# Probabilities divided on VectorE instead of GpSimd, and GELU of three gates after their eviction

## The chip, the cores and the metric

The kernel runs on one core of one Trainium2 chip. The metric is the device time of one execution in microseconds (us). Before the change the median of three executions is 2908.08 us (2890.9 to 2912.65). The kernel's engines are TensorE (PE; PEld is its weight load), VectorE (DVE), ScalarE (ACT), GpSimd (POOL) and SyncE (SP), which issues nearly all DMAs.

## The reference

The program computes four residual steps on 4 batches of 512 tokens with 128 features each: attention with 16 small heads, a stack of six layers, a second attention, and a routed mixture of experts. The change lies in the stack of layers (`DEPTH = 6`). What a layer computes, cut to what matters:

```
for i in range(DEPTH):
    x = attn_layer(shift_tokens(x), Wqkv[i], q_scale[i], k_scale[i], Wo[i]) + x
    x = ffn_layer(shift_tokens(x), ln_g[i], ln_b[i], W1[i], b1[i], W2[i], b2[i]) + x

attn_layer: q, k, v = split(x @ Wqkv)              # 16 heads of 64
            q = l2norm(q) * qs;  k = l2norm(k) * ksc
            q, k = rotated with cos, sin and a scale by position
            sim = q @ k.T * 8 within a window of 32 tokens and the one ahead of it
            out = softmax(sim) @ v;  return out @ Wo
ffn_layer:  xn = layernorm(x) * g + bln
            a, gate = split(xn @ W1 + b1)          # 341 columns each
            return a * gelu(gate, exact) @ W2 + b2
```

## The kernel before

**Tiles, slots and rounds.** In the layers the work is cut into tiles T of 128 tokens: four tiles (`TILES`) make one batch entry, four entries one layer, so 6 x 4 x 4 = 96 tiles. Every engine runs a list of 96 *slots*, one for each tile, written out by hand (`layer_slots`): the slots of the first two entries and of the last two stand alone, the 16 slots of a layer between them are the body of a loop that runs five times. Here the four slots of one entry are called a *round*, and slot 0 to slot 3 are its slots by `i`. The engines meet through semaphores that count up.

**What a slot does.** In slot T the attention of tile T is scored while tile T+1 is rotated and normalised, tile T+2 is projected and tile T-1 is weighed. By engine, in program order:

- PE: turns the keys and queries of tile T (`turn_keys`, `turn_queries`, L866, L881), mixes values (L929), `scores(T)` (mask L888, scores L898), projects tile T+2 (L855), mixes again, `weigh(T-1)` (L919, reads the turned probabilities in `sc`), `turn_windows` (L911).
- DVE: `square_sums(T+1)` (L1552, L1553), `turn_probs(T-1)` (L1601, a transpose of 128x1024), `turn_plain(T+1)` (L1558, waits for both products of `turn_swapped(T+1)` on POOL), `add_queries(T+1)` (L1563), `softmax(T)` (L1579 the maxima, L1584 the difference, both read PSUM), `scaled(T+1, 0)` (L1573), `sums(T)` (L1589 and the reciprocal L1594), `scaled(T+1, 1)` (L1573).
- ACT: copies keys and queries (L1284, L1288), `guess(T+1)` (L1276, L1279, after L1553), `exponentials(T)` (L1292, after L1584), `take(T+2)` (L1262, two halves out of PSUM), `squares(T+2)` (L1270), `weighed(T-1)` (L1301), `windows` (L1306).
- POOL: a small copy (L606), `inverse_root(T+1)` (L585 to L588, after the guess), `add_keys(T+1)` (L593), `normalise(T)` (L598, waits for the reciprocal L1594), `turn_swapped(T+2)` (L576, L577, waits for `take(T+2)`).

Two tiles of probabilities lie in `sc[:, 0]` and `sc[:, 1]`; the turned ones in `sc[:, 2]`.

**The feed-forward part** of an entry is spread over the slots of a round two rounds later. PE multiplies three chunks of gate columns (`gate`, L958; chunk 0 at the end of slot 0, chunks 1 and 2 in slot 1 ahead of `scores`) into one and the same PSUM bank 7, so each waits until ACT has evicted the one before. ACT evicts them with the GELU itself (L1323), and the table of functions is switched for it and back (ACT_TABLE_LOAD, L1323 and L1361 in slot 0, L1323 and L1344 in slot 1). The three plain chunks (`plain`, L966) follow through the same bank, each waiting for DVE's `hidden` of the one before (L1639): `plain(0)` and `plain(1)` in slot 1 ahead of and behind `weigh`, `plain(2)` in slot 2 ahead of `scores`. On DVE `hidden(0)` and `hidden(1)` close slot 1, `hidden(2)` stands ahead of `softmax` in slot 2, whose end holds L1644 and L1621; slot 0 has the layer norm's scale (L1629, L1633) behind `softmax`, slot 3 its centring (L303). `gate(1)` and `gate(2)` stand on ACT behind `guess`.

Of the kernel before, what the change touches and what calls it, by code (L numbers as in the profile page):

```python
# [20 lines left out]
P = 128  # L21
# [57 lines left out]
def build(nc, I, out):  # L79
    with ExitStack() as ctx:  # L80
# [3 lines left out]
        def sem(name):  # L84
            return ctx.enter_context(nc.semaphore(name))
# [119 lines left out]
        def projections(a, b):  # L205
# [42 lines left out]
            sem(n) for n in ("l_xt", "l_xe", "l_px", "l_pc", "l_mm", "l_mw", "l_m", "l_res", "l_xf", "l_fn"))  # L248
        f_h, f_g, f_hd, f_y = sem("f_h"), sem("f_g"), sem("f_hd"), sem("f_y")

# [275 lines left out]
        def _(pool):  # L526
# [67 lines left out]

            def normalise(T, i):
                pool.wait_ge(l_rd, T + 1)
                p3 = probs(i).rearrange("p (h j) -> p h j", j=64)
                pool.tensor_tensor(p3, p3, rden(i).unsqueeze(2).broadcast_to([P, LH, 64]), ALU.mult).then_inc(l_pn, 1)  # L598

            def slot(it, l, b, i, ahead):  # L600
# [6 lines left out]
                if ahead >= 1:  # L607
                    inverse_root(T + 1, (i + 1) % 2)
                    add_keys(T + 1, (i + 1) % 2)
                normalise(T, i)  # L610
                if ahead >= 2:
# [38 lines left out]
        def _(pe):  # L650
# [263 lines left out]
            def weigh(T, i):  # L914

                p4 = sc[:, 2, :].rearrange("p (h v t) -> p h v t", h=LH, v=2)
                for half in range(2):
# [218 lines left out]
        def _(act):  # L1136
# [183 lines left out]
            def gate(j, n):  # L1320
                m = FCH[n][1]
                act.wait_ge(f_h, 6 * j + n + 1)
                act.activation(gates[0:m, n, :], bank[0:m, 7, :], ACT.Gelu, bias=lb[0:m, 6 + n:7 + n]).then_inc(f_g, 1)  # L1323

# [5 lines left out]
            def slot(it, l, b, i, ahead):  # L1330
# [10 lines left out]
                if i == 1 and feeds:  # L1341
                    gate(it - 2, 1)
                    gate(it - 2, 2)
                    act.preload_act_table_set("natural_log_exp_and_others")  # L1344
                exponentials(T, i)
# [13 lines left out]
                if i == 0 and feeds:  # L1359
                    gate(it - 2, 0)  # L1360
                    act.preload_act_table_set("natural_log_exp_and_others")  # L1361
                if i == 0 and not (isinstance(it, int) and it == LAST):
# [23 lines left out]
            for n in range(3):  # L1386
                gate(LAST - 1, n)
            act.preload_act_table_set("natural_log_exp_and_others")
            shift_ffn(LAST, BATCH - 1)
            ln_squares(act, LAYER0 + LAST)  # L1390
            layer_root(LAST)
            for n in range(3):
                gate(LAST, n)
            act.preload_act_table_set("natural_log_exp_and_others")
            attention(1)
# [22 lines left out]
        def _(dve):  # L1418
# [168 lines left out]
            def sums(T, i):  # L1587
# [6 lines left out]
                dve.reciprocal(rden(i), u_den).then_inc(l_rd, 1)  # L1594

            def turn_probs(T, i):
                if not (isinstance(T, int) and T == 0):
                    dve.wait_ge(l_px, 2 * T)
                dve.wait_ge(l_pn, T + 1)
                settle(dve)  # L1600
                dve.transpose(sc[:, 2, :], probs(i)).then_inc(l_pt, 1)  # L1601

# [32 lines left out]
            def hidden(j, n):  # L1635
                m = FCH[n][1]
                dve.wait_ge(f_h, 6 * j + n + 4)
                dve.wait_ge(f_g, 3 * j + n + 1)
                dve.scalar_tensor_tensor(out=hT[0:m, n, :], in0=bank[0:m, 7, :], scalar=lb[0:m, 3 + n:4 + n],  # L1639
# [7 lines left out]
            def slot(it, l, b, i, ahead):  # L1647
# [5 lines left out]
                if ahead >= 1:  # L1653
                    square_sums(T + 1, (i + 1) % 2)
                if not (first and i == 0):
                    turn_probs(T - 1, (i - 1) % 2)
                if ahead >= 1:
# [14 lines left out]
                if ahead >= 1:  # L1672
                    scaled(T + 1, (i + 1) % 2, 1)
                if i == 1 and feeds:
                    hidden(it - 2, 0)
                    hidden(it - 2, 1)
# [12 lines left out]
            layer_slots(dve, slot)  # L1689
            turn_probs(DEPTH * BATCH * TILES - 1, 1)  # L1690
            scale_norm(LAST - 1, DEPTH - 1)
# [168 lines left out]
```

## Time and profile before

| | before |
|---|---|
| median of three executions | 2908.08 us (2890.9 to 2912.65) |
| the profiled execution | 2895.91 us, span 2894.1 us |
| busy: PE, DVE, ACT, POOL | 2220.3, 1948.6, 1536.6, 1470.0 us |
| granted TensorE clock, mean | 0.893 |
| slots of the layers, first to last reciprocal | 423 to 2248 us of the span |

The layers are about 1830 us of the span, the rest belongs to the two attentions and the experts, which the change leaves alone. A row of a timeline gives start and length in us, engine, line, operation, output<-input, the count of merged instructions, and in brackets the engine's idle time before it with what ended it.

### The profile page before, as it was taken

The numbers are of one execution on the slowest core, as the hardware profiler recorded it, in microseconds if no ns is written. First come the engines' busy times: TensorE is split into PE (matmuls) and PEld (weight loads), VectorE is DVE, ScalarE is ACT, GpSimd is POOL, SyncE is SP. The second block draws the span as 40 slices with busy tenths as digits, with TensorE's granted clock in tenths as the row PEclk, the third lists the DMA queues.
The fourth block names the chain that finished last, engine by engine and source line by source line (L and its number), as shares of the span: only waits on it lengthen the run. The fifth ranks groups of instructions, "written<-read, shape, count | busy, mean of one in ns | idle before, by whom it ended". The sixth has DMA issues, their size and how long they took to land.

```text
span 2894.1 us, 53763 instructions
## 1 busy us (share of the span) xinstructions
PE 2220.3 (77%) x21684; PEld 1186.8 (41%) x21780; DVE 1948.6 (67%) x2087; ACT 1536.6 (53%) x1859; POOL 1470.0 (51%) x1031
## 2 busy tenths in 40 slices
PE   4678758788888888888888888888888756788253
PEld 1111124455555455545555555545555311112253
DVE  2676457888778878787778887887877246763101
ACT  2255745665666666656656665666665223546100
POOL 5500047776676667666667766766766153000202
PEclk8698989999999999999999999999999766989686
DMA  5100000000010000000010001000000010000122
GB/s 154 50 21 26 1 1 16 1 2 16 1 25 2 16 1 10 16 16 1 1 25 1 16 2 25 2 16 1 9 2 1 0 60 32 23 23 16 41 76 65
DMA packets 55828, 59.08 MB, mean 20 GB/s; under 512 B 13142, under 2 KB 45012, under 8 KB 55508
## 3 DMA queue, kind: packets, MB, share of 16 engines
q1 hardware_dynamic: 53444, 50.77, 5.9%
q0 software_dynamic: 2128, 4.72, 0.7%
q8 instruction: 182, 2.98, 0.5%
q14 instruction: 74, 0.61, 0.1%
HBM read 44.07 MB, written 11.01 MB: 19 GB/s over the span
## 4 chain that ended last, share of the span: by engine, by line
PE 47%; issue 13%; ACT 13%; POOL 12%; DVE 11%; DMA 2%; SPq 1%; POOLq 0%; ACTq 0%; DVEq 0%
PE bank L855 7%; PE bank L929 6%; PE bank L919 5%; PE bank L731 5%; PE bank L702 4%; DVE big L1452 3%; PE bank L898 3%; ACT pxs L1301 2%; POOL big L576 2%; POOL big L593 2%; ACT L1323 2%; PE bank L958 2%; POOL big L577 2%; ACT big L1176 2%; PE bank L966 2%
## 5 line engine op out<-in xcount | busy, mean ns | idle before, releaser
L598 POOL TENSOR_TENSOR sc<-sc,small 128x1024 f32<-128x1024 f32 x96 | 263.4, 2744 | 467.3 <-DVE small L1594 467.3
L1452 DVE TENSOR_REDUCE big<-bank 128x1 f32<-128x512 f32 x512 | 328.6, 685 | 199.1 <-PE bank L702 194.8
L1292 ACT ACTIVATE sc<-sc 128x1024 f32<-128x1024 f32 x96 | 101.5, 1057 | 532.2 <-DVE sc L1584 532.2
L855 PE MATMUL bank<-wqk,xs 128*128 128x512 f32 x768 | 364.8, 617 | 13.4 <-ACT xs L1257 8.3
L929 PE MATMUL bank<-pxs,mw 128*128 128x256 f32 x1536 | 366.2, 382 | 0.0
L929 PEld LDWEIGHTS bank<-pxs,mw 128*128 128x128 f32 x1536 | 291.1, 192 | 100.9 <-issue 70.3
L1176 ACT ACTIVATE big<-bank 128x1024 f32<-128x1024 f32 x256 | 250.1, 1026 | 139.6 <-PE bank L716 136.8
L1558 DVE TENSOR_TENSOR big<-big,rotCl 128x2048 f32<-128x2048 f32 x96 | 222.4, 2317 | 79.2 <-POOL big L577 79.2
L702 PE MATMUL bank<-pxs 48*128 48x512 bf16 x512 | 186.1, 445 | 116.1 <-DVE big L1452 72.1
L1552 DVE TENSOR_REDUCE small<-big 128x32 f32<-128x2048 f32 x96 | 219.0, 2281 | 38.2 <-ACT big L1270 28.5
L1573 DVE TENSOR_TENSOR big<-big,small 128x1024 f32<-128x1024 f32 x192 | 241.0, 1256 | 1.1 <-POOL small L588 1.1
L919 PE MATMUL bank<-sc,xnat 32*128 32x512 f32 x1536 | 200.8, 637 | 41.9 <-ACT big L1262 39.0
L576 POOL TENSOR_TENSOR big<-big,rotSl 128x1024 f32<-128x1024 f32 x96 | 226.9, 2364 | 8.3 <-ACT big L1262 8.2
L577 POOL TENSOR_TENSOR big<-big,rotSl 128x1024 f32<-128x1024 f32 x96 | 227.5, 2370 | 0.0
L593 POOL TENSOR_TENSOR big<-big 128x1024 f32<-128x1024 f32 x96 | 226.2, 2356 | 0.0
L1579 DVE TENSOR_REDUCE small<-bank 128x16 f32<-128x1024 f32 x96 | 116.9, 1218 | 142.5 <-PE bank L898 142.5
L855 PEld LDWEIGHTS bank<-wqk,xs 128*128 128x128 f32 x768 | 142.6, 196 | 168.1 <-issue 160.9
L1301 ACT ACTIVATE pxs<-bank 128x1024 f32<-128x1024 f32 x192 | 185.7, 1020 | 39.9 <-PE bank L919 36.5
L958 PE MATMUL bank<-xc,w 128*128 128x512 f32 x144 | 102.4, 800 | 119.4 <-ACT gates L1323 116.5
L1270 ACT ACTIVATE big<-big 128x2048 f32<-128x2048 f32 x96 | 183.3, 1910 | 11.5 <-DVE small L1553 1.1
L1262 ACT ACTIVATE big<-bank 128x1024 f32<-128x1024 f32 x192 | 184.8, 1011 | 5.3 <-PE bank L855 5.2
L702 PEld LDWEIGHTS bank<-pxs 48*128 48x128 bf16 x512 | 40.5, 95 | 356.4 <-DVE big L1452 267.7
(237 smaller groups left out, 4035.4 us busy)
## 6 DMA issues: line engine op xcount, KB each, us to landing
wqk<-in_L_ffn_w SPq DMA_DIRECT2D x32, 256.0 KB, 3.1
wqk<-in_L_ffn_Wqkv SPq DMA_DIRECT2D x12, 512.0 KB, 4.3
pxs<-part_rows SPq DMA_DIRECT2D x64, 96.0 KB
pxs<-part_rows SPq DMA_DIRECT2D x64, 64.0 KB
wvt<-in_wv_layers_t SPq DMA_DIRECT2D x6, 512.0 KB, 5.1
wol<-in_L_ffn_Wo SPq DMA_DIRECT2D x6, 512.0 KB, 5.5
part_rows<-big SPq DMA_DIRECT2D x24, 128.0 KB
part_rows<-sc SPq DMA_DIRECT2D x24, 128.0 KB
```

The lines of the kernel that those rows point to most:

```text
L576: pool.tensor_tensor(r4[:, :, :, 0:h], q4[:, :, :, h:], tab[:, :, :, 0:h], ALU.mult).then_inc(l_rb, 1)
L577: pool.tensor_tensor(r4[:, :, :, h:], q4[:, :, :, 0:h], tab[:, :, :, h:], ALU.mult).then_inc(l_rb, 1)
L593: pool.tensor_tensor(raws(i)[:, INNER:], raws(i)[:, INNER:], rotB[:, INNER:], ALU.add).then_inc(l_ak, 1)
L598: pool.tensor_tensor(p3, p3, rden(i).unsqueeze(2).broadcast_to([P, LH, 64]), ALU.mult).then_inc(l_pn, 1)
L702: pe.matmul(bank[:, 4 + r, :], qst[64 * r:64 * r + MAX_ROW, b % 2, p, qt * P:(qt + 1) * P], kst[64 * r:64 * r + MAX_ROW, b % 2, p, :], sta ...
L855: m = pe.matmul(bank[:, 2 - 2 * half + c, :], xs[:, b % 2, WIN + i * P:WIN + (i + 1) * P], wqk[:, (2 * half + c) * 512:(2 * half + c + 1) ...
L919: m = pe.matmul(bank[:, (4, 5, 2, 3)[w], :], xnat[32 * w:32 * w + 32, i % 2, half, :], p4[32 * w:32 * w + 32, :, half, :], start=(half == ...
L929: m = pe.matmul(bank[:, 6, part * 2 * P:(part + 1) * 2 * P], mw[:, 2 * (a % 4) + s, a // 4, :], pxs[:, part, a, s, :], start=(a == 0 and s ...
L1176: act.activation(pT[:, u % 2, 2 * half:2 * half + 2, :], bank[:, q:q + 2, :], ACT.Exp).then_inc(a_p, 1)
L1301: act.activation(pxs[:, i // 2, :, :, t:t + 64].rearrange("p c r (w t) -> p w (c r) t", w=2), bank[:, 4 - 2 * half:6 - 2 * half, :].rearra ...
L1452: dve.tensor_reduce(nm[:, qt, 2 * p + r:2 * p + r + 1], bank[:, 4 + r, :], AX.X, ALU.max, negate=True).then_inc(a_mx, 1)
L1573: dve.tensor_tensor(r3, r3, nrm(i)[:, half * LH:(half + 1) * LH].unsqueeze(2).broadcast_to([P, LH, LD]), ALU.mult).then_inc((l_yq, l_yk)[h ...
```

## The change

It has two parts. First, `normalise(T)` goes from POOL, where it stood between `add_keys(T+1)` and `turn_swapped(T+2)`, to DVE, behind `scaled(T+1, 1)`; `turn_probs(T)` follows at once, in slot T instead of slot T+1, into one of two buffers (`sc[:, 2 + i % 2]`). Second, ACT evicts each gate chunk with Identity and its bias, without a table switch, and a new function `gelus` applies GELU from SBUF to SBUF to two chunks at once and to the third, between two table loads, in slot 1 behind `gate(2)` and ahead of `exponentials`; `hidden` waits for it by a new semaphore.

```diff
--- before.py
+++ after.py
@@ -246,7 +246,7 @@
             sem(n) for n in ("l_s", "l_mx", "l_e", "l_p", "l_dn", "l_rd", "l_pn", "l_pt"))
         l_xt, l_xe, l_px, l_pc, l_mm, l_mw, l_m, l_res, l_xf, l_fn = (
             sem(n) for n in ("l_xt", "l_xe", "l_px", "l_pc", "l_mm", "l_mw", "l_m", "l_res", "l_xf", "l_fn"))
-        f_h, f_g, f_hd, f_y = sem("f_h"), sem("f_g"), sem("f_hd"), sem("f_y")
+        f_h, f_g, f_ge, f_hd, f_y = sem("f_h"), sem("f_g"), sem("f_ge"), sem("f_hd"), sem("f_y")
 
         m_lg, m_sh, m_ex, m_oh, m_cum, m_ch, m_idx = (
             sem(n) for n in ("m_lg", "m_sh", "m_ex", "m_oh", "m_cum", "m_ch", "m_idx"))
@@ -592,11 +592,6 @@
                 pool.wait_ge(l_rb, 2 * T + 2)
                 pool.tensor_tensor(raws(i)[:, INNER:], raws(i)[:, INNER:], rotB[:, INNER:], ALU.add).then_inc(l_ak, 1)
 
-            def normalise(T, i):
-                pool.wait_ge(l_rd, T + 1)
-                p3 = probs(i).rearrange("p (h j) -> p h j", j=64)
-                pool.tensor_tensor(p3, p3, rden(i).unsqueeze(2).broadcast_to([P, LH, 64]), ALU.mult).then_inc(l_pn, 1)
-
             def slot(it, l, b, i, ahead):
 
                 T = it * TILES + i
@@ -607,7 +602,6 @@
                 if ahead >= 1:
                     inverse_root(T + 1, (i + 1) % 2)
                     add_keys(T + 1, (i + 1) % 2)
-                normalise(T, i)
                 if ahead >= 2:
                     if b == BATCH - 1 and i == 2:
                         pool.wait_ge(l_tab, 3 * l + 6)
@@ -913,7 +907,7 @@
 
             def weigh(T, i):
 
-                p4 = sc[:, 2, :].rearrange("p (h v t) -> p h v t", h=LH, v=2)
+                p4 = sc[:, 2 + i % 2, :].rearrange("p (h v t) -> p h v t", h=LH, v=2)
                 for half in range(2):
                     for w in range(4):
                         m = pe.matmul(bank[:, (4, 5, 2, 3)[w], :], xnat[32 * w:32 * w + 32, i % 2, half, :],
@@ -1320,7 +1314,15 @@
             def gate(j, n):
                 m = FCH[n][1]
                 act.wait_ge(f_h, 6 * j + n + 1)
-                act.activation(gates[0:m, n, :], bank[0:m, 7, :], ACT.Gelu, bias=lb[0:m, 6 + n:7 + n]).then_inc(f_g, 1)
+                act.activation(gates[0:m, n, :], bank[0:m, 7, :], ACT.Identity, bias=lb[0:m, 6 + n:7 + n]).then_inc(f_g, 1)
+
+            def gelus(j):
+
+                act.wait_ge(f_g, 3 * j + 3)
+                settle(act)
+                act.activation(gates[:, 0:2, :], gates[:, 0:2, :], ACT.Gelu).then_inc(f_ge, 1)
+                act.activation(gates[0:FCH[2][1], 2, :], gates[0:FCH[2][1], 2, :], ACT.Gelu).then_inc(f_ge, 1)
+                act.preload_act_table_set("natural_log_exp_and_others")
 
             def mixed_weights(l, half):
                 act.wait_ge(l_mm, 2 * l + half + 1)
@@ -1341,7 +1343,7 @@
                 if i == 1 and feeds:
                     gate(it - 2, 1)
                     gate(it - 2, 2)
-                    act.preload_act_table_set("natural_log_exp_and_others")
+                    gelus(it - 2)
                 exponentials(T, i)
                 if ahead >= 2:
                     take(T + 2, i % 2, 0)
@@ -1358,7 +1360,6 @@
                     layer_root(it - 1)
                 if i == 0 and feeds:
                     gate(it - 2, 0)
-                    act.preload_act_table_set("natural_log_exp_and_others")
                 if i == 0 and not (isinstance(it, int) and it == LAST):
                     if first or second or (isinstance(it, int) and it == 2):
                         act.wait_ge(step_done, LAYER0 + 1)
@@ -1385,13 +1386,13 @@
                 weighed(N - 1, LAST, TILES - 1, half)
             for n in range(3):
                 gate(LAST - 1, n)
-            act.preload_act_table_set("natural_log_exp_and_others")
+            gelus(LAST - 1)
             shift_ffn(LAST, BATCH - 1)
             ln_squares(act, LAYER0 + LAST)
             layer_root(LAST)
             for n in range(3):
                 gate(LAST, n)
-            act.preload_act_table_set("natural_log_exp_and_others")
+            gelus(LAST)
             attention(1)
             norm_all_scalar(act, MOE0)
             act.wait_ge(m_tk, 1)
@@ -1593,12 +1594,17 @@
                 settle(dve)
                 dve.reciprocal(rden(i), u_den).then_inc(l_rd, 1)
 
+            def normalise(T, i):
+                dve.wait_ge(l_rd, T + 1)
+                p3 = probs(i).rearrange("p (h j) -> p h j", j=64)
+                dve.tensor_tensor(p3, p3, rden(i).unsqueeze(2).broadcast_to([P, LH, 64]), ALU.mult).then_inc(l_pn, 1)
+
             def turn_probs(T, i):
-                if not (isinstance(T, int) and T == 0):
-                    dve.wait_ge(l_px, 2 * T)
+                if not (isinstance(T, int) and T < 2):
+                    dve.wait_ge(l_px, 2 * T - 2)
                 dve.wait_ge(l_pn, T + 1)
                 settle(dve)
-                dve.transpose(sc[:, 2, :], probs(i)).then_inc(l_pt, 1)
+                dve.transpose(sc[:, 2 + i % 2, :], probs(i)).then_inc(l_pt, 1)
 
             def tables(l):
 
@@ -1635,7 +1641,7 @@
             def hidden(j, n):
                 m = FCH[n][1]
                 dve.wait_ge(f_h, 6 * j + n + 4)
-                dve.wait_ge(f_g, 3 * j + n + 1)
+                dve.wait_ge(f_ge, 2 * j + (1, 1, 2)[n])
                 dve.scalar_tensor_tensor(out=hT[0:m, n, :], in0=bank[0:m, 7, :], scalar=lb[0:m, 3 + n:4 + n],
                                          in1=gates[0:m, n, :], op0=ALU.add, op1=ALU.mult).then_inc(f_hd, 1)
 
@@ -1652,8 +1658,6 @@
                 more = not (isinstance(l, int) and l == DEPTH - 1)
                 if ahead >= 1:
                     square_sums(T + 1, (i + 1) % 2)
-                if not (first and i == 0):
-                    turn_probs(T - 1, (i - 1) % 2)
                 if ahead >= 1:
                     turn_plain(T + 1, (i + 1) % TILES)
                     add_queries(T + 1, (i + 1) % 2)
@@ -1671,6 +1675,8 @@
                 sums(T, i)
                 if ahead >= 1:
                     scaled(T + 1, (i + 1) % 2, 1)
+                normalise(T, i)
+                turn_probs(T, i)
                 if i == 1 and feeds:
                     hidden(it - 2, 0)
                     hidden(it - 2, 1)
@@ -1687,7 +1693,6 @@
             scaled(0, 0, 0)
             scaled(0, 0, 1)
             layer_slots(dve, slot)
-            turn_probs(DEPTH * BATCH * TILES - 1, 1)
             scale_norm(LAST - 1, DEPTH - 1)
             for n in range(3):
                 hidden(LAST - 1, n)
```

On DVE, at the end of slot 1 (`hidden` writes `hT`; the second L1573 of a slot is `scaled(T+1, 1)`), before:

```order
L1573 TENSOR_TENSOR big<-big,small 128x1024
L1637 ISA
L1638 ISA
L1639 SCALAR_TENSOR_TENSOR hT<-bank,lb,gates 128x512
L1637 REGISTER_ALU
L1638 REGISTER_ALU
L1639 SCALAR_TENSOR_TENSOR hT<-bank,lb,gates 128x512
L1548 REGISTER_ALU
L1552 TENSOR_REDUCE small<-big 128x32
L1553 TENSOR_SCALAR small<-small 128x32
L1601 STREAM_TRANSPOSE sc<-sc 128x1024
```

and now, from the same `scaled(T+1, 1)`, which is L1574 there:

```order
L1574 TENSOR_TENSOR big<-big,small 128x1024
L1600 TENSOR_TENSOR sc<-sc,small 128x1024
L1604 REGISTER_ALU
L1607 STREAM_TRANSPOSE sc<-sc 128x1024
L1643 ISA
L1644 REGISTER_ALU
L1645 SCALAR_TENSOR_TENSOR hT<-bank,lb,gates 128x512
L1643 REGISTER_ALU
L1645 SCALAR_TENSOR_TENSOR hT<-bank,lb,gates 128x512
L1549 REGISTER_ALU
L1553 TENSOR_REDUCE small<-big 128x32
```

The division L1600 and the transpose L1607 (before L1601, behind L1553 of the next slot) stand directly behind the second scaling and ahead of both `hidden`.

On POOL, from `add_keys` to the next small copy, before:

```order
L593 TENSOR_TENSOR big<-big 128x1024
L598 TENSOR_TENSOR sc<-sc,small 128x1024
L568 ISA
L576 TENSOR_TENSOR big<-big,rotSl 128x32x32
L577 TENSOR_TENSOR big<-big,rotSl 128x32x32
L604 ISA
L606 COPY kbuf<-kbuf 128x8x32
```

and now:

```order
L593 TENSOR_TENSOR big<-big 128x1024
L568 ISA
L576 TENSOR_TENSOR big<-big,rotSl 128x32x32
L577 TENSOR_TENSOR big<-big,rotSl 128x32x32
L601 COPY kbuf<-kbuf 128x8x32
```

L598 is gone, so that the two products of `turn_swapped` follow `add_keys` with only their own wait between (L568, for `take`).

On ACT, in slot 1, from the guess (`small`) over the evictions of gate chunks 1 and 2 to the exponentials (`sc`), before:

```order
L1276 ACTIVATE small<-small 128x32
L1279 ACTIVATE small<-small 128x32
L1322 REGISTER_ALU
L1323 ACT_TABLE_LOAD
L1323 ACTIVATE gates<-bank,lb 128x512
L1322 REGISTER_ALU
L1323 ACTIVATE gates<-bank,lb 85x512
L1344 ACT_TABLE_LOAD
L1292 ACTIVATE sc<-sc 128x1024
```

and now:

```order
L1270 ACTIVATE small<-small 128x32
L1273 ACTIVATE small<-small 128x32
L1316 REGISTER_ALU
L1317 ACTIVATE gates<-bank,lb 128x512
L1316 REGISTER_ALU
L1317 ACTIVATE gates<-bank,lb 85x512
L1321 REGISTER_ALU
L1323 ACT_TABLE_LOAD
L1323 ACTIVATE gates<-gates 128x1024
L1324 ACTIVATE gates<-gates 85x512
L1325 ACT_TABLE_LOAD
L1286 ACTIVATE sc<-sc 128x1024
```

The loads now frame the two GELUs behind the last eviction. In slot 0 the two loads around the eviction of chunk 0 (L1323 and L1361) are gone without a replacement.

## Rows read from the trace of the kernel before

**Rows 1.** Busy time of the engines in the layers: stretch, its length, busy us (instructions), granted clock

```profile
core 0: us, PE busy (x) PEld busy (x) DVE busy (x) ACT busy (x) POOL busy (x), PEclk, DMA share, GB/s
420.00:2250.00 1830.00, 1547.99 (x18403) 936.57 (x18497) 1474.02 (x1237) 1144.10 (x1368) 1257.71 (x826) 0.95 0.03 9
```

**Rows 2.** Timeline of DVE in one round, slot 0 to slot 3

```profile
1411.99 1.22 DVE L1579 TENSOR_REDUCE small<-bank 128x16 f32<-128x1024 f32 x1
...
1419.02 1.16 DVE L1573 TENSOR_TENSOR big<-big,small 128x1024 f32<-128x1024 f32 x1
...
1435.76 1.22 DVE L1579 TENSOR_REDUCE small<-bank 128x16 f32<-128x1024 f32 x1 [5.55 <-PE bank L898]
...
1445.70 0.75 DVE L1639 SCALAR_TENSOR_TENSOR hT<-bank,lb,gates 128x512 f32<-128x512 f32 x1 [2.81 <-PE bank L966]
...
1454.16 1.21 DVE L1579 TENSOR_REDUCE small<-bank 128x16 f32<-128x1024 f32 x1
...
1459.45 1.16 DVE L1573 TENSOR_TENSOR big<-big,small 128x1024 f32<-128x1024 f32 x1
1460.53 0.74 DVE L1644 SCALAR_TENSOR_TENSOR zT<-bank,lb,zT 128x512 f32<-128x512 f32 x1
...
1461.91 2.29 DVE L1552 TENSOR_REDUCE small<-big 128x32 f32<-128x2048 f32 x1
...
1464.64 1.23 DVE L1601 STREAM_TRANSPOSE sc<-sc 128x1024 f32<-128x1024 f32 x1
1467.04 2.29 DVE L1558 TENSOR_TENSOR big<-big,rotCl 128x2048 f32<-128x2048 f32 x1 [1.17 <-POOL big L577]
...
1470.51 1.22 DVE L1579 TENSOR_REDUCE small<-bank 128x16 f32<-128x1024 f32 x1
...
1473.05 1.69 DVE L1573 TENSOR_TENSOR big<-big,small 128x1024 f32<-128x1024 f32 x1
...
1476.81 1.16 DVE L1573 TENSOR_TENSOR big<-big,small 128x1024 f32<-128x1024 f32 x1
```

**Rows 3.** Timeline of DVE, the maxima of slot 3 and slot 0, a round later

```profile
1549.56 1.22 DVE L1579 TENSOR_REDUCE small<-bank 128x16 f32<-128x1024 f32 x1
...
1567.10 1.22 DVE L1579 TENSOR_REDUCE small<-bank 128x16 f32<-128x1024 f32 x1
```

**Rows 4.** Timeline of POOL in the same round as rows 2

```profile
1459.62 2.75 POOL L598 TENSOR_TENSOR sc<-sc,small 128x1024 f32<-128x1024 f32 x1 [3.31 <-DVE small L1594]
...
1471.31 2.35 POOL L593 TENSOR_TENSOR big<-big 128x1024 f32<-128x1024 f32 x1
```

**Rows 5.** Timeline of ACT in the same round, slots 1 and 2

```profile
1428.59 0.23 ACT L1279 ACTIVATE small<-small 128x32 f32<-128x32 f32 x1
1428.84 1.28 ACT L1323 ACT_TABLE_LOAD   x1
1430.13 0.69 ACT L1323 ACTIVATE gates<-bank,lb 128x512 f32<-128x512 f32 x1
...
1438.41 1.06 ACT L1292 ACTIVATE sc<-sc 128x1024 f32<-128x1024 f32 x1 [3.52 <-DVE sc L1584]
...
1457.77 1.92 ACT L1262 ACTIVATE big<-bank 128x1024 f32<-128x1024 f32 x2
```

**Rows 6.** Timeline of PE, gate chunk 2 and the scores of slot 1

```profile
1430.88 2.00 PE L958 MATMUL bank<-xc,w 128*85 128x512 f32 x2 [4.30 <-ACT gates L1323]
...
1433.66 2.06 PE L898 MATMUL bank<-kbuf,qT 64*32 64x64 f32 x128
```

**Rows 7.** Timeline of all engines but PE, ahead of the first slot

```profile
404.92 2.34 POOL L593 TENSOR_TENSOR big<-big 128x1024 f32<-128x1024 f32 x1
404.99 6.60 DVE L1573 TENSOR_TENSOR big<-big,small 128x1024 f32<-128x1024 f32 x2 [1.11 <-POOL small L588]
407.43 3.09 POOL L576 TENSOR_TENSOR big<-big,rotSl 128x1024 f32<-128x1024 f32 x1 [0.17 <-POOL big L593]
410.48 3.33 POOL L577 TENSOR_TENSOR big<-big,rotSl 128x1024 f32<-128x1024 f32 x1
```

## The prediction

> **What bounds the kernel now.** I read the busy time of the layers first, then the timelines of DVE, POOL, ACT and PE over one round of four slots. In the layers PE is busy 1548 us of 1830 and DVE 1474 [rows 1]; neither is full, so a loop through several engines sets the pace, and the timeline must show which. I mark a slot by the start of its maxima on DVE (L1579). The round shown has them at 1411.99, 1435.76, 1454.16 and 1470.51 [rows 2]: slot 0 to 1 takes 23.77 us, 1 to 2 takes 18.40, 2 to 3 takes 16.35; slot 3 to 0 takes 17.54 in a later round (1567.10-1549.56) [rows 3]. Together 76.1 us; 24 rounds of that would be 1826, the layers' 1830.
>
> The loop is: reciprocal on DVE, division on POOL (L598, 2.75 us [rows 4]), POOL's two products behind it (L576, L577), then on DVE L1558, which waits 1.17 us for them [rows 2], L1563, the maxima, and so to the next reciprocal. In slot 0 to 1 another wait ends last: DVE waits 5.55 us for the scores [rows 2], PE having waited 4.30 us for the eviction of gate chunk 1 [rows 6], which stood on ACT behind the guess and a table load of 1.28 us [rows 5].
>
> **Part one: the division on DVE.** POOL is relieved of 2.75 us a slot [rows 4]. On DVE the division is like L1573, the same shape with a broadcast factor: 1.16 us [rows 2]. The transpose stays 1.23 us. DVE gains 96 x 1.16 = 111 us of work, and its total in the layers, 1474+111 = 1585, still fits into 1830. The question is what both do to the loop.
>
> POOL's products no longer wait for the division; they wait for `take(T+2)`, which ends in slot 2 at 1457.77+1.92 = 1459.69, that is 5.53 us behind the slot's maxima [rows 2, 5]. With 0.18 us for the semaphore (L576 idled 0.17 us behind L593's end [rows 7]) L576 is ready at +5.71. Just there DVE runs the second L1573 (+5.29 to +6.45 in slot 2, +6.30 in slot 3, +7.03 in slot 0 [rows 2]) and then the division. All three read two operands from SBUF, and the trace shows that such operations of DVE and POOL exclude each other. Ahead of the first slot two L1573 stand back to back while POOL has L593, L576 and L577 to do [rows 7]: the two take 6.60 us instead of 2.3, L576 3.09 and L577 3.33 instead of 2.35. The ends fit one order only: L593 to 407.26, L1573 to about 408.33, L576 to 410.52, L1573 to 411.59, L577 to 413.81. So they take turns, an operation waiting on one engine goes in between two of the other, a blocked product ends 2.19 us behind the release (410.52-408.33) and a blocked L1573 1.07 us (411.59-410.52). The 1.69 us of L1573 at 1473.05, beside L593 [rows 2, 4], is the same in small (1473.66+1.08).
>
> The Trainium skill (SBUF — State Buffer, section "SBUF: two separate sides") says that a VectorE operation with two SBUF inputs and a GpSimd operation that reads SBUF lock each other out for a whole instruction. The trace agrees, with the 6.60 us.
>
> So, counted from the maxima, with 0.17 us between division and transpose and the pipeline's small overlaps:
>
> - *Slot 2 to 3.* L1573 to 6.45, L576 in between to 8.64, division to 9.71, transpose to 11.1, L1644 and L1621 1.38 (1461.91-1460.53) to 12.5, L1552 and L1553 2.6 (2.73 before, 1464.64-1461.91, with L576 of POOL beside them), then 3.47 from L1558 to the maxima (1470.51-1467.04): 18.5, before 16.35. POOL's L577 ends at 11.9 and is waited for no more.
> - *Slot 3 to 0.* L576 is first (5.71 to 8.06), L1573 to 9.13, L577 to 11.3, division to 12.4, transpose to 13.8, 2.6 and 3.47: 19.8, before 17.54.
> - *Slot 1 to 2.* As slot 2 up to the transpose at 11.1; `hidden(0)` to 11.8; only then PE can run `plain(1)`, for which I take 1.1 (half of what gate chunk 2 took after idle time, 2.00 [rows 6]); `hidden(1)` to 13.7; 2.6, 3.47 and `hidden(2)` 0.7: 20.3, before 18.40. The wait of 2.81 us in front of the second L1639 [rows 2] shrinks, but is not gone.
> - The eight slots of the first two rounds have no gates and less beside them. Between nothing and slot 2's +2.2 I take +1.5 each, 12 us in all.
>
> Without these locks the same sums give 16.5, 16.1 and 18.4: even then the DVE, now serial, would gain little in slots 1 and 2.
>
> **Part two: the gates.** In slot 0 ACT loses two loads of 1.28 us; it then stands idle instead, since the guess waits for L1553. With the division in front, slot 0 runs: L576 from 5.71, L1573 (due at 7.03) to 9.13, L577 to 11.3, division 12.4, transpose 13.8, L1552 and L1553 to 16.4. Then the guess (two short ACTIVATEs, 0.23 us one [rows 5]) to 17.1, and the eviction of chunk 1 (0.69, no load ahead of it) to 17.85. From its end to the maxima the rows give 1435.76-1430.82 = 4.94 us [rows 2, 5], with PE slow after its idle time (2.00 us for two matmuls of chunk 2, 2.06 for the scores [rows 6]); PE idles about as long again, so I keep it: 22.8, before 23.77. Of the 3.85 us of loads that left this chain 1.0 is kept, the division's way has taken the rest. The GELUs follow the last eviction: 1.28, 1.06 (as the exponentials of the same size, L1292), 0.69 and 1.28 make 4.3 us, and the eviction itself 0.69. From the end of gate chunk 2 (1432.88) to L1292 (1438.41) there are 5.53 us [rows 5, 6]; they hide there, and would cost exponentials and all behind them up to 1.5 us if the scores ran at the full clock.
>
> The load's price is where the page and the row differ. Behind the load of 1.28 us the eviction starts at once, 1430.13 after 1428.84+1.28 [rows 5]. The Trainium skill (ScalarE: Activation LUTs, section "What ACT_TABLE_LOAD costs") adds a drain of about 1380 ns to each switch; with it the load ahead of chunk 1 would be worth 1.4 us more, 30 us over 22 rounds. The row decides: 1.28.
>
> **The sum.** A round goes from 76.1 to 22.8+20.3+18.5+19.8 = 81.4. That is +5.3; a few rounds are longer than the one shown (24 x 76.1 stays 4 us under 1830) and have some cover of their own, so I take +5. 22 rounds with gates: +110; the first two: +12. Profiled execution 2896+122 = 3018. The median of before lies 12 us above that execution; I say 3020.
>
> **Rivals.**
> 1. *Faster.* The locks don't bite: L576 gets ready only after the division (it would have to come 1.9 us later, beyond +7.6), or DVE is served first. For it: POOL's start is by a hop from another place. Against it: rows 7. Round: 16.5+16.1+18.4, and slot 0 with its division done at 9.35 gives 19.8: 70.8, -5.3; times 22, with a few for the start: 2775. If only every second lock bites (DVE passes both its operations at one turn) about 2830. Chance 17%.
> 2. *Nearly nothing.* The gates give more: PE's gap ahead of chunk 2 gets short enough that it stays at the full clock, 1.8 us less a round, and one of the three lock terms is lost: 81.4-1.8-2.2 = 77.4, +29 us over 22 rounds: 2930. Chance 11%.
> 3. *Slower still.* PE idles 282 of 1830 us now and would idle about 400 of 1950, and its clock, 0.95 as a mean in the layers [rows 1], falls; the scores of slot 1 were slow after an idle time of 4.30 us [rows 6]. If slots 0 and 1 lose 1 to 2 us each to it: 3065 to 3100. Or slots 1 and 2 fall into the order of slot 3, their L1573 only 0.42 us ahead of L576: +2.2 each, 3115. Chance 14%.
>
> The forecast itself, 2940 to 3050, has 58%. The range, 2860 to 3090, leaves out most of rival 1 and the far end of rival 3. Differences under 1% (2879 to 2937) are about what a measurement can't tell from none: faster 0.17, same 0.11, slower 0.72.
>
> **What would show it.** Each step has its row: the division on DVE with 2.2 to 3.3 us instead of 1.16; L576 starting some 5.7 us behind the maxima and L577 or L576 at about 3.3; slots of 22.8, 20.3, 18.5, 19.8; no wait of DVE for L577; ACT idle ahead of the guess of slot 1; the second `hidden` waiting about 1 us. A division of 1.2 us throughout would make it wrong at its main step.

## The result and the profile after

The changed kernel takes 2990.47 us as a median (2984.79 to 3002.68, four executions), the kernel before 2903.66 in its four: a ratio of 1.031, 95% interval 1.026 to 1.036. The forecast was 3020 (2860 to 3090), slower. The profiled execution took 2984.79 us with a span of 2983.0, 88.9 more than before.

The layers, in the view that answers to [rows 1] (stretch, length, busy us and instructions of each engine, granted clock):

```profile
core 0: us, PE busy (x) PEld busy (x) DVE busy (x) ACT busy (x) POOL busy (x), PEclk, DMA share, GB/s
420.00:2337.00 1917.00, 1576.81 (x18472) 959.62 (x18471) 1741.62 (x1330) 1118.18 (x1364) 1115.20 (x735) 0.93 0.03 9
```

VectorE is busy 1742 us where it was busy 1474. That is 268 more for 96 divisions which, at their own length (1.21 us in a run below), are worth 116. The groups in the page's list (busy us, mean ns of one) tell where the rest lies:

```profile
L1600 DVE TENSOR_TENSOR sc<-sc,small 128x1024 f32<-128x1024 f32 x96 | 319.7, 3331 | 0.0
L1574 DVE TENSOR_TENSOR big<-big,small 128x1024 f32<-128x1024 f32 x192 | 292.2, 1522 | 1.1 <-POOL small L588 1.1
L577 POOL TENSOR_TENSOR big<-big,rotSl 128x1024 f32<-128x1024 f32 x96 | 319.4, 3328 | 0.0
L576 POOL TENSOR_TENSOR big<-big,rotSl 128x1024 f32<-128x1024 f32 x96 | 264.6, 2756 | 311.4 <-ACT big L1256 311.2
```

Of the kernel before:

```profile
L1573 DVE TENSOR_TENSOR big<-big,small 128x1024 f32<-128x1024 f32 x192 | 241.0, 1256 | 1.1 <-POOL small L588 1.1
L1553 DVE TENSOR_SCALAR small<-small 128x32 f32<-128x32 f32 x96 | 98.1, 1022 | 3.3
```

The divisions hold 320-116 = 204 us of it, and the scalings (L1574) 51 us more than before. The total grows by less than that, because a small operation, L1553 (now L1554), fell from 98 to 18 us: a collision that the kernel before had is gone. Its rows in slot 0 of the round in [rows 2], DVE and then POOL, show that it ends with GpSimd's first product:

```profile
1422.40 1.86 DVE L1553 TENSOR_SCALAR small<-small 128x32 f32<-128x32 f32 x1
```

```profile
1421.90 2.33 POOL L576 TENSOR_TENSOR big<-big,rotSl 128x1024 f32<-128x1024 f32 x1
```

In the kernel before, 91 of the 96 L1553 take over 0.3 us (0.18 where nothing holds one), and 89 of these end 0.03 to 0.05 us behind the end of one of GpSimd's operations on `big`. So a second SBUF tensor is not the only thing that makes a VectorE operation collide: this one reads one tensor and two constants.

The timeline of slot 2 of the changed kernel, DVE and then POOL (L1580 is the maxima, before L1579; L1574 the second scaling, before L1573), answers to [rows 2, 4]:

```profile
1509.59 1.22 DVE L1580 TENSOR_REDUCE small<-bank 128x16 f32<-128x1024 f32 x1
...
1514.91 1.16 DVE L1574 TENSOR_TENSOR big<-big,small 128x1024 f32<-128x1024 f32 x1
1515.99 3.37 DVE L1600 TENSOR_TENSOR sc<-sc,small 128x1024 f32<-128x1024 f32 x1
1519.50 1.25 DVE L1607 STREAM_TRANSPOSE sc<-sc 128x1024 f32<-128x1024 f32 x1
...
1527.78 1.22 DVE L1580 TENSOR_REDUCE small<-bank 128x16 f32<-128x1024 f32 x1
```

```profile
1515.21 3.06 POOL L576 TENSOR_TENSOR big<-big,rotSl 128x1024 f32<-128x1024 f32 x1 [2.90 <-ACT big L1256]
1518.23 3.34 POOL L577 TENSOR_TENSOR big<-big,rotSl 128x1024 f32<-128x1024 f32 x1
```

L576 arrives at +5.62 behind the maxima, while L1574 runs to 1516.07 (+6.48). It ends at 1518.27, the division at 1519.36 (+9.77), L577 at 1521.57. The prediction had 5.71, 6.45, 8.64, 9.71 and 11.9 for these.

Between the maxima of slot 0 and slot 1 the gates' part shows, on ACT and on PE of the changed kernel (L1270 and L1273 are the guess, L1317 the evictions, L952 gate chunk 2, L892 the scores), which answers to [rows 5, 6]:

```profile
1482.96 0.23 ACT L1270 ACTIVATE small<-small 128x32 f32<-128x32 f32 x1 [2.87 <-DVE small L1554]
1483.31 0.23 ACT L1273 ACTIVATE small<-small 128x32 f32<-128x32 f32 x1
1483.45 0.67 ACT L1317 ACTIVATE gates<-bank,lb 128x512 f32<-128x512 f32 x1
...
1486.99 1.28 ACT L1323 ACT_TABLE_LOAD   x1
1488.29 1.06 ACT L1323 ACTIVATE gates<-gates 128x1024 f32<-128x1024 f32 x1
1489.25 0.61 ACT L1324 ACTIVATE gates<-gates 85x512 f32<-85x512 f32 x1
1489.88 1.28 ACT L1325 ACT_TABLE_LOAD   x1
1491.18 1.06 ACT L1286 ACTIVATE sc<-sc 128x1024 f32<-128x1024 f32 x1
```

```profile
1484.17 2.00 PE L952 MATMUL bank<-xc,w 128*85 128x512 f32 x2 [3.78 <-ACT gates L1317]
1485.97 1.06 PE L882 MATMUL bank<-maskr,maskw 128*128 128x512 bf16 x2
1486.95 1.48 PE L892 MATMUL bank<-kbuf,qT 64*32 64x64 f32 x128
```

The load ahead of chunk 1 is gone, yet PE idles 3.78 us for it, after 4.30 before. The guess in front of the eviction comes no earlier, although ACT has lost the two loads of slot 0: it ends 17.0 us behind the maxima before and 16.9 now (means of 22 rounds). Before, ACT itself was late; VectorE's sum of squares, which the guess needs, had ended at 12.2. Now that sum ends at 16.2, behind the blocked division, and ACT stands idle for it (2.87 us in the first row).

The time of a slot, from one start of the maxima to the next, worked out from the starts of all 96 (means over the 21 whole rounds from the third one on):

| slot | before | after | change | predicted |
|---|---|---|---|---|
| 0 to 1 | 23.75 | 21.36 | -2.4 | -1.0 |
| 1 to 2 | 19.03 | 22.09 | +3.1 | +1.9 |
| 2 to 3 | 16.60 | 18.35 | +1.8 | +2.2 |
| 3 to 0 | 18.34 | 19.99 | +1.6 | +2.3 |
| round | 77.7 | 81.8 | +4.1 | +5.3, taken as +5 |

21 rounds make +85 us, the first eight slots +4.6, the last three +2.2: 92. What lies around the layers is 3 us shorter in the after trace, which I leave as the difference of two executions.

### The profile page after: what moved, and what is told of

The parts are those of the page before. It is cut to its first block and busy times, and to the rows that moved or that the text cites. A ratio compares the mean times of both kernels' runs of the same rounds, so it can differ in the third digit from the quotient of the medians.

```text
span 2983.0 us, 53967 instructions
## 1 busy us (share of the span) xinstructions
PE 2249.5 (75%) x21780; PEld 1207.7 (40%) x21780; DVE 2216.0 (74%) x2183; ACT 1517.6 (51%) x1863; POOL 1323.4 (44%) x935
## 5 line engine op out<-in xcount | busy, mean ns | idle before, releaser
L576 POOL TENSOR_TENSOR big<-big,rotSl 128x1024 f32<-128x1024 f32 x96 | 264.6, 2756 | 311.4 <-ACT big L1256 311.2
L1600 DVE TENSOR_TENSOR sc<-sc,small 128x1024 f32<-128x1024 f32 x96 | 319.7, 3331 | 0.0
L577 POOL TENSOR_TENSOR big<-big,rotSl 128x1024 f32<-128x1024 f32 x96 | 319.4, 3328 | 0.0
L1574 DVE TENSOR_TENSOR big<-big,small 128x1024 f32<-128x1024 f32 x192 | 292.2, 1522 | 1.1 <-POOL small L588 1.1
L913 PE MATMUL bank<-sc,xnat 32*128 32x512 f32 x1536 | 210.6, 665 | 71.8 <-ACT big L1256 69.7
L585 POOL TENSOR_TENSOR small<-small 128x32 f32<-128x32 f32 x96 | 125.7, 1310 | 268.3 <-ACT small L1273 268.3
L1553 DVE TENSOR_REDUCE small<-big 128x32 f32<-128x2048 f32 x96 | 217.0, 2260 | 20.7 <-ACT big L1264 11.8
L1559 DVE TENSOR_TENSOR big<-big,rotCl 128x2048 f32<-128x2048 f32 x96 | 221.6, 2308 | 0.0
L960 PE MATMUL bank<-xc,w 128*128 128x512 f32 x144 | 98.0, 769 | 90.8 <-DVE hT L1645 89.3
```

The source lines that it names most:

```text
L576: pool.tensor_tensor(r4[:, :, :, 0:h], q4[:, :, :, h:], tab[:, :, :, 0:h], ALU.mult).then_inc(l_rb, 1)
L577: pool.tensor_tensor(r4[:, :, :, h:], q4[:, :, :, 0:h], tab[:, :, :, h:], ALU.mult).then_inc(l_rb, 1)
L1553: ch.link(dve.tensor_reduce(ss, sq.rearrange("p (h d) -> p h d", d=LD), AX.X, ALU.add))
L1559: dve.tensor_tensor(r4, r4, rotCl[:, i % TILES, :].rearrange("p (a d) -> p a d", a=2).unsqueeze(2).broadcast_to([P, 2, LH, LD]), ALU.mult) ...
L1574: dve.tensor_tensor(r3, r3, nrm(i)[:, half * LH:(half + 1) * LH].unsqueeze(2).broadcast_to([P, LH, LD]), ALU.mult).then_inc((l_yq, l_yk)[h ...
L1600: dve.tensor_tensor(p3, p3, rden(i).unsqueeze(2).broadcast_to([P, LH, 64]), ALU.mult).then_inc(l_pn, 1)
```

## Experiments

All times are medians of four executions, ratios go against the kernel before on the same chip. The runs stood on several chips, where the kernel before takes 2897 to 2904 us, so that times of different runs can be set side by side to about 0.2%.

**The division alone.** The gates are left as before; the diff is against the kernel before and leaves out the second buffer for the turned probabilities, which this run has too.

```diff
             def normalise(T, i):
-                pool.wait_ge(l_rd, T + 1)
+                dve.wait_ge(l_rd, T + 1)
                 p3 = probs(i).rearrange("p (h j) -> p h j", j=64)
-                pool.tensor_tensor(p3, p3, rden(i).unsqueeze(2).broadcast_to([P, LH, 64]), ALU.mult).then_inc(l_pn, 1)
+                dve.tensor_tensor(p3, p3, rden(i).unsqueeze(2).broadcast_to([P, LH, 64]), ALU.mult).then_inc(l_pn, 1)
...
-                if not (first and i == 0):
-                    turn_probs(T - 1, (i - 1) % 2)
...
+                normalise(T, i)
+                turn_probs(T, i)
```

> The division and the transpose on VectorE as in the changed kernel, the gates as before (GELU in the eviction, four table loads a round). Theory (the division collides with GpSimd's two products, the gates help): slot 0 to 1 gets the load of 1.28 us ahead of chunk 1 back, and the longer wait of TensorE behind it, so 22.6 to 24 us there instead of 21.4 in the changed kernel, the other slots as in it (22.1, 18.4, 20.0): 30 to 55 us over the changed kernel's 2990, so 3020 to 3045, ratio to before 1.040 to 1.050. Rival (the gate function is what costs, since GELU from SBUF delays the exponentials of slot 1): faster than the changed kernel, near or under 2960.

Measured: 3056.56 us, ratio 1.057 (1.052 to 1.062), a little beyond what the theory gave and on the other side of the rival. Slots 24.1, 21.6, 18.7, 20.0. So this half of the change is worse by itself, by 5.7%. The two halves do not simply add up: slot 0 to 1 differs by 2.7 us from the changed kernel, not by 1.2 to 2.6, as ACT, with four loads in its queue, becomes late again ahead of the guess (it ends at 17.5 behind the maxima, against 16.9) and PE idles 4.30 us instead of 3.5 (means of the rounds).

**The gates alone.** Division on GpSimd, transpose a slot later, as before; `gelus` and Identity as in the change.

The diff is against the kernel before.

```diff
-                act.activation(gates[0:m, n, :], bank[0:m, 7, :], ACT.Gelu, bias=lb[0:m, 6 + n:7 + n]).then_inc(f_g, 1)
+                act.activation(gates[0:m, n, :], bank[0:m, 7, :], ACT.Identity, bias=lb[0:m, 6 + n:7 + n]).then_inc(f_g, 1)
...
-                    act.preload_act_table_set("natural_log_exp_and_others")
+                    gelus(it - 2)
...
-                    act.preload_act_table_set("natural_log_exp_and_others")
...
-                dve.wait_ge(f_g, 3 * j + n + 1)
+                dve.wait_ge(f_ge, 2 * j + (1, 1, 2)[n])
```

> The new gate function alone, the division on GpSimd and the transpose a slot later, as before. Theory: slot 0 to 1 loses 3.85 us of table loads ahead of the eviction of chunk 1 and then the slow clock of TensorE too, 23.75 to 18 or 20 us; the other slots stay (19.0, 16.6, 18.3). 22 rounds of -3.7 to -5.6: 2780 to 2825, ratio 0.957 to 0.973. Rival (the loads were hidden, the gain of the gates is small as in the changed kernel): -1 to -2 us a round, 2865 to 2885.

Measured: 2797.52 us, ratio 0.965 (0.963 to 0.968). The slots are 18.5, 19.4, 16.6 and 18.3: all of the gain is in slot 0 to 1, -5.3 us. ACT and PE of this kernel in that slot:

```profile
1312.43 0.23 ACT L1279 ACTIVATE small<-small 128x32 f32<-128x32 f32 x1
1312.56 0.67 ACT L1323 ACTIVATE gates<-bank,lb 128x512 f32<-128x512 f32 x1
1314.41 0.68 ACT L1323 ACTIVATE gates<-bank,lb 85x512 f32<-85x512 f32 x1 [1.18 <-PE bank L958]
```

```profile
1313.29 1.09 PE L958 MATMUL bank<-xc,w 128*85 128x512 f32 x2 [1.28 <-ACT gates L1323]
1314.21 0.59 PE L888 MATMUL bank<-maskr,maskw 128*128 128x512 bf16 x2
1314.74 1.49 PE L898 MATMUL bank<-kbuf,qT 64*32 64x64 f32 x128
```

PE waits 1.28 us instead of 4.30, and after so short a wait the two matmuls of chunk 2 take 1.09 us instead of 2.00 and the scores 1.49 instead of 2.06 [rows 6]. The granted clock in those stretches is 1.00 here (1313.20 to 1314.40 and 1314.70 to 1316.30) and was 0.50 before (1430.80 to 1432.90 and 1433.60 to 1435.80), the higher and the lower of TensorE's two levels, 2.4 and 1.2 GHz. This kernel beats both: the change is 3.1% slower, its second half alone 3.5% faster.

**The same length of work without a second SBUF input.** The division is left out and a reduction of the same tile stands in its place; the probabilities stay undivided, so the result is not that of the layers.

```diff
-                dve.tensor_tensor(p3, p3, rden(i).unsqueeze(2).broadcast_to([P, LH, 64]), ALU.mult).then_inc(l_pn, 1)
+                dve.tensor_reduce(small[:, 1, LH:2 * LH], p3, AX.X, ALU.add).then_inc(l_pn, 1)
```

> The changed kernel with the division replaced by a reduction of the same tile (128x1024 to 128x16, 1.2 us), so the probabilities stay undivided: the same length of VectorE work at the same place, but one SBUF input instead of two. Theory (port shared with GpSimd): the operation takes 1.2 us and not 3.3; slots about 19.7, 19.0, 16.4, 17.6 instead of 21.4, 22.1, 18.4, 20.0, so some 9 us a round less: near 2790, ratio 0.95 to 0.97. Rival (the slower time is the serial work that VectorE took on, 2.4 us a slot, whatever its inputs): within 1% of the changed kernel, 2960 to 3020.

Measured: 2798.28 us, ratio 0.965 (0.963 to 0.968), 192 us less than the changed kernel, for a work of the same length at the same place of the same engine. Slots 18.6, 19.2, 16.9, 18.3. Its timeline, DVE and POOL, around a reduction in the division's place (L1600):

```profile
1342.89 1.76 DVE L1574 TENSOR_TENSOR big<-big,small 128x1024 f32<-128x1024 f32 x1
1344.58 1.21 DVE L1600 TENSOR_REDUCE small<-sc 128x16 f32<-128x1024 f32 x1
1345.92 1.25 DVE L1607 STREAM_TRANSPOSE sc<-sc 128x1024 f32<-128x1024 f32 x1
```

```profile
1341.20 2.37 POOL L576 TENSOR_TENSOR big<-big,rotSl 128x1024 f32<-128x1024 f32 x1 [4.01 <-ACT big L1256]
1343.51 3.36 POOL L577 TENSOR_TENSOR big<-big,rotSl 128x1024 f32<-128x1024 f32 x1
```

L1574, with two SBUF inputs, is still held by L576 (to 1343.57) and ends 1.08 us behind it, and L577 is held by L1574 in turn. L1574 as a whole takes 288 us here, against 292. The reduction and the transpose run through beside L577 in 1.21 and 1.25 us.

**One wait more.** The change itself, but GpSimd's products wait for the division.

```diff
+                    pool.wait_ge(l_pn, T + 1)
                     turn_swapped(T + 2, (i + 2) % TILES)
```

> The changed kernel with one wait more: GpSimd starts its two products only when the division of the same tile is done. Theory (collision): the division falls to 1.2 us, the products run beside the transpose and the sum of squares, and though they start 2 us later, slots are about 20, 18.4, 16.4, 17.2: 72 against 81.8 us a round, near 2780 to 2800, ratio 0.955 to 0.97. Rival (the loop over GpSimd sets the pace, a wait more on it lengthens it by the 1.9 us that it delays the products): 96 slots of up to 1.9 us more, 3050 to 3170.

Measured: 2800.09 us, ratio 0.966 (0.962 to 0.970), with all the work of the changed kernel in it and a wait added. Slots 18.9, 18.9, 16.8, 18.5: the round, 73.1, is near the 72 expected, but slot 0 came out 1.1 us shorter and slot 3 1.3 us longer than expected. GpSimd is idle 584 us for the division (second row), and neither the products nor the division are blocked any more; groups by line of this kernel:

```profile
L577 POOL TENSOR_TENSOR big<-big,rotSl 128x1024 f32<-128x1024 f32 x96 | 227.7, 2372 | 0.0
L576 POOL TENSOR_TENSOR big<-big,rotSl 128x1024 f32<-128x1024 f32 x96 | 227.5, 2370 | 592.4 <-DVE sc L1601 584.1 <-ACT big L1257 8.2 <-POOL big L593 0.2
```

```profile
L1601 DVE TENSOR_TENSOR sc<-sc,small 128x1024 f32<-128x1024 f32 x96 | 116.3, 1211 | 0.0
```

**Who comes first.** A shorter wait: for the second scaling only.

```diff
+                    pool.wait_ge(l_yk, T + 2)
                     turn_swapped(T + 2, (i + 2) % TILES)
```

> The changed kernel with GpSimd's two products waiting only for the second scaling on VectorE (L1574), which ends 0.7 us behind the projections' eviction, and no longer for the division. Theory (turns by order of arrival): the semaphore reaches GpSimd some 0.17 us after VectorE has gone on to the division, so the division has the port first and takes 1.2 us, the first product is held up for about 1 us instead, and the two start 1 us earlier than with the wait for the division. Slots as there or a little shorter (18.7, 18.8, 16.6, 18.2): 2775 to 2800, ratio 0.955 to 0.967. Rival (what helped there was the later start of the products as such, not who comes first): between the changed kernel and that one, 2850 to 2950, with divisions of 2 us and more.

Measured: 2795.96 us, ratio 0.963 (0.959 to 0.967). Slots 18.5, 19.2, 17.0, 18.2. The scaling's end releases GpSimd, but VectorE goes on at once; DVE and POOL of this kernel:

```profile
1354.35 1.16 DVE L1575 TENSOR_TENSOR big<-big,small 128x1024 f32<-128x1024 f32 x1
1355.43 1.21 DVE L1601 TENSOR_TENSOR sc<-sc,small 128x1024 f32<-128x1024 f32 x1
```

```profile
1355.77 3.09 POOL L576 TENSOR_TENSOR big<-big,rotSl 128x1024 f32<-128x1024 f32 x1 [7.38 <-DVE big L1575]
```

L576 comes 0.34 us behind the start of the division and is the one that is held, 3.09 us instead of 2.37; the division keeps its 1.21, as in all 96 slots (1.21 to 1.23; L576 comes 0.16 to 0.35 us behind its start). In the changed kernel L576 came 0.7 us or more ahead of the division, and 94 of the 96 divisions took 3.35 to 3.40 us.

In both kernels with a wait, half of the small operations behind the sum of squares (L1555, L1553 before) are held by the products again, 0.75 and 0.58 us as a mean against 0.18 in the changed kernel. And both take what the gates alone take, 2797.52 us: with the collision of the division removed, the move itself is worth nothing measurable. What these waits gain, they gain over the changed kernel.

**The order in slot 1.** The changed kernel with `hidden(0)` and `hidden(1)` ahead of the division.

```diff
+                if i == 1 and feeds:
+                    hidden(it - 2, 0)
+                    hidden(it - 2, 1)
                 normalise(T, i)
                 turn_probs(T, i)
-                if i == 1 and feeds:
-                    hidden(it - 2, 0)
-                    hidden(it - 2, 1)
```

> The changed kernel with the two hidden operations of slot 1 ahead of the division and the transpose instead of behind them, the same work in another order. Theory (in slot 1 the blocked division also makes hidden(0) late, and TensorE idles 3.8 us ahead of plain chunk 1 and is slow behind it): TensorE's wait for hidden(0) goes, the division falls beside the end of GpSimd's second product, and slot 1 to 2 takes 20 to 21 us instead of 22.1; the other slots stay. 22 rounds of -1.1 to -2: 2945 to 2970, ratio 1.015 to 1.025. Rival (the order around hidden does not matter, since VectorE is busy all the same): 2980 to 3000.

Measured: 2965.23 us, ratio 1.023 (1.018 to 1.028). Slot 1 to 2 takes 20.4 us instead of 22.1, the others 21.7, 18.3 and 20.0. The whole is 25 us shorter than the changed kernel, but the two ratios, 1.018 to 1.028 and 1.026 to 1.036, just overlap, so the reading rests on the slot. PE, changed kernel first and this one second, at plain chunk 1 (L960) and what follows:

```profile
1500.35 1.83 PE L960 MATMUL bank<-xc,w 128*128 128x512 f32 x2 [3.76 <-DVE hT L1645]
1501.97 0.63 PE L905 MATMUL bank<-ident,xs 128*128 128x128 f32 x2
1502.40 1.85 PE L860 MATMUL bank<-ident,big 128*128 128x128 f32 x8
```

```profile
1476.19 1.12 PE L960 MATMUL bank<-xc,w 128*128 128x512 f32 x2
1477.46 0.44 PE L905 MATMUL bank<-ident,xs 128*128 128x128 f32 x2
1477.73 1.04 PE L860 MATMUL bank<-ident,big 128*128 128x128 f32 x8
```

The granted clock in these stretches, the changed kernel first and this one second:

```profile
core 0: us, PE busy (x) PEld busy (x) DVE busy (x) ACT busy (x) POOL busy (x), PEclk, DMA share, GB/s
1500.30:1502.20 1.90, 1.85 (x4) 0.76 (x5) 0.00 (x0) 0.00 (x0) 0.16 (x1) 0.59 0.00 0
1476.10:1477.40 1.30, 1.21 (x6) 0.30 (x2) 0.05 (x1) 1.02 (x2) 1.30 (x2) 1.00 0.00 0
```

The wait of 3.76 us and the slow operations behind it are gone, and the granted clock (PEclk) is 1.00 instead of 0.59.

**What binds at 2796.** Three kernels that do the whole work end there. This one has the wait for the scaling and no division at all; it leaves the probabilities undivided.

```diff
-                dve.tensor_tensor(p3, p3, rden(i).unsqueeze(2).broadcast_to([P, LH, 64]), ALU.mult).then_inc(l_pn, 1)
+                dve.tensor_copy(small[:, 1, LH:2 * LH], rden(i)).then_inc(l_pn, 1)
```

> The kernel with the products behind the second scaling, and the division left out (a copy of 128x16 in its place, the probabilities stay undivided): 1.1 us less for VectorE in each slot. Three kernels that are unlike each other (gates alone, products behind the division, products behind the scaling) take 2796 to 2800. If that is a common bound outside the division (TensorE with ScalarE's eviction of the weighed values, TensorE being busy 88% there), this one lies within 1% of them: 2770 to 2800, ratio 0.953 to 0.965. If VectorE's serial work is the bound, 96 x 1.1 = 106 us less: 2690 to 2720.

Measured: 2720.94 us, ratio 0.939 (0.935 to 0.942), 75 us less. Of 106 us of work 75 came off the end, so VectorE's serial work binds most slots of that kernel, and my guess of a common bound outside the division was wrong. Leaving out the division also frees GpSimd's first product (2.37 us as a mean instead of 3.11), but VectorE never waits for the products in either kernel (L1560, 0.0 us idle), so the 75 us do not come from a wait for them. That the three meet at 2796 to 2800 is then by chance as far as these runs go; in the kernel with the gates alone VectorE has that work less and loses it to GpSimd instead: it waits 79 us in all for the second product, and its small operation behind the sum of squares takes 1.20 us as a mean, 115 us in all.

## Why the prediction was right, and where its terms were off

**The locks** between VectorE's operations with two SBUF inputs and GpSimd's products were right as a mechanism and in size. Replacing the second SBUF input, or letting the products start later, each takes 190 to 195 us off the changed kernel without shortening VectorE's own work. The rule of turns, read from one place ahead of the first slot [rows 7], held in the layers: an operation that waits goes in between two of the other engine. Slot 2 was forecast to within 0.2 us (18.5 against 18.35), and so was slot 3 (19.8 against 19.99). VectorE no longer waits for GpSimd's second product, as forecast: 0.0 us ahead of L1559, where it waited 79 us in all before. What the prediction did not see is that the kernel before had a collision of its own, that of L1553: it priced L1552 and L1553 at 2.6 us for every slot, and behind the change they take 2.4.

**The sum** came out closer than its terms. The round was forecast at 81.4 us and takes 81.8, but slot 0 came out 1.4 us shorter and slot 1 1.8 us longer than forecast, and these cancel by luck. And the round before was taken at 76.1 us and takes 77.7; checking it as 24 x 76.1 = 1826 against 1830 could not show that, since the first two rounds, without gates, take only 69 us each.

**Slot 3 to 0** was off as a difference, +1.6 instead of +2.3, since its base was. I took 17.54 from the round after the one shown; the round shown itself takes 20.85 there (maxima at 1470.51 and 1491.36), and the mean before is 18.34, over 17.2 to 20.8. What makes the long ones is not shown. +5 instead of +5.3 gave back too little of it. A base for a sum has to be the mean over all rounds.

**Slot 0 to 1** gained 2.4 and not 1.0. In the round shown the guess came at the time I had (ends at 1483.54, +16.9; I had 17.1), but from the end of the eviction to the maxima it took 1488.48-1484.12 = 4.36 us and not 4.94: PE was slow for chunk 2 (granted clock 0.50 from 1484.10 to 1486.20) and back at its full rate for the scores (1.48 us; 0.98 from 1486.90 to 1488.50). As a mean of 22 rounds that stretch takes 3.9 us. The experiment with the gates alone shows the rest of this term: with a wait of 1.28 us none of the operations behind it is slow. The other rounds of that slot take 20.5 to 22.4 us.

**Slot 1 to 2** lost 3.1 and not 1.9. The wait of PE for `hidden(0)` was forecast, its price was not: 1.83 us for plain chunk 1, where I had 1.1, and slow transposes behind it (1.85 instead of 1.04), all behind an idle time of 3.76 us and at a granted clock of 0.59. VectorE's second `hidden` waits 1.92 us for it, where I had 1.0. So the slot's length was missed by 1.8 us (20.3 against 22.09), the difference by 1.2 only, because the base was too low here too, 18.40 in the round shown and 19.03 as a mean. The run with `hidden` first took 1.7 us off this slot. That was half of rival 3, the clock, and it did occur in this place. The row of that wait:

```profile
1502.22 0.75 DVE L1645 SCALAR_TENSOR_TENSOR hT<-bank,lb,gates 128x512 f32<-128x512 f32 x1 [1.92 <-PE bank L960]
```

**The first eight slots** cost 4.6 us in all where I had 12. Four of them take 0.4 to 0.7 us more than before, near the lower end of the span that I had given, nothing to +2.2, three take 1.2 to 1.9 more, and one takes 1.6 less.

**The gates' loads.** I forecast that the division's way eats most of what the gates give, 1.0 us kept of 3.85. By the runs the gates' part is worth 3.5% alone and about 2.6 points of the ratio behind the division (1.057 to 1.031). The GELUs hid for the most part. In the round shown the exponentials start at 1491.18, right behind the second load and 0.08 us after L1585 had ended (1489.88+1.22), which they need in any case; the usual distance is 0.03. In 10 of the 22 rounds they start 0.5 us behind L1585, held by the load, which is the small form of the 1.5 us that the prediction named. DVE in that slot:

```profile
1489.88 1.22 DVE L1585 TENSOR_TENSOR sc<-bank,small 128x1024 f32<-128x1024 f32 x1 [0.18 <-DVE small L1580]
```

No load to GELU was followed by a gap: the GELU starts 0.01 to 0.02 us behind it, and the load itself starts at most 0.11 us behind the eviction in these rounds. So the drain that the Trainium skill counts with each switch (ScalarE: Activation LUTs, section "What ACT_TABLE_LOAD costs") does not show here either.

**Rivals.** The faster one (no locks) is refuted for the change as it is, and it is what the runs with the added wait made of it. Its gain was priced too high: 2775 forecast for no locks, 2796 to 2800 measured.

## What to carry to other kernels

Before moving an operation with two SBUF inputs to VectorE, look at what GpSimd does at that time: here each such pair that met cost the later one the rest of the other. Ask who arrives first; a wait that makes the less urgent engine come a moment later was worth 6% of this kernel. Then compare with the kernel without the move: here the repaired move (2796 and 2800) and no move at all (2797.5) came out the same. And two edits that touch one loop are to be measured apart: here the one cost 5.7%, the other gave 3.5%, and together they looked like one bad idea.

## What the runs showed that I had not expected

- An operation's time in the profile contains its wait for the other engine: the division shows 3.33 us "busy" and no idle time before it, and VectorE as a whole 1742 us busy in the layers, of which 204 are waiting in the divisions alone. A busy share of 91% (1742 of 1917) was not a full engine.
- The order of arrival decides over 2.2 us of length: L576 0.34 us behind the start of the division leaves it at 1.21 us, L576 0.78 us ahead of it makes it 3.37.
- The granted clock in the layers has a mean of 0.93 in the changed kernel against 0.95 [rows 1], and 0.97 to 0.99 from 420 to 2100 us in the five fastest kernels, where PE's wait for chunk 1 is 1.1 to 2.0 us as a mean instead of 3.5 and 4.2.
